# One ScalarE step of a mixture-of-experts kernel in another order: where the first part of new expert weights is split

## What is computed

```python
g = jax.lax.ragged_dot(x_sorted, we_gate, group_sizes)
u = jax.lax.ragged_dot(x_sorted, we_up, group_sizes)
o = jax.lax.ragged_dot(jax.nn.silu(g) * u, we_down, group_sizes)
w_sorted = topk_w.reshape(-1)[sort].astype(o.dtype)
y = jnp.zeros_like(x_flat).at[tok].add(o * w_sorted[:, None])
```

## Time and profile before

| | us |
|---|---|
| median of 3 runs | 3972.36 (3971.4 to 3972.74) |
| the profiled execution, as timed | 3973.47 |
| its span in the trace | 3971.7 |
| TensorE matmul busy | 3650.4 (92%) |
| VectorE busy | 2313.6 (58%) |
| ScalarE busy | 1349.9 (34%) |
| GpSimd busy | 1602.0 (40%) |

### The profile page before, as it was taken

One profiled execution on the slowest core, in us unless ns is written; L12 is line 12 of the kernel. 1 busy time (PEld: TensorE's weight loads), 2 busy tenths in 40 slices (PEclk: granted clock), 3 DMA queues, 4 the chain that ended last, 5 costly groups with the idle time before them and its releaser, 6 DMA issues.

```text
span 3971.7 us, 110141 instructions
## 1 busy us (share of the span) xinstructions
PE 3650.4 (92%) x16856; PEld 2774.8 (70%) x16857; DVE 2313.6 (58%) x5802; ACT 1349.9 (34%) x4031; POOL 1602.0 (40%) x1208
## 2 busy tenths in 40 slices
PE   6809999967999999999999999999999999999996
PEld 3404445536877777787778778787888777787785
DVE  5364555555666665656665565656555666666653
ACT  2212222213333433434333343334333343334331
POOL 1010000004555555555555455555555555455443
PEclk9959999988999999999999999999999999999998
DMA  3322323225666676667666666666666676666654
GB/s 113 106 61 86 98 97 98 96 56 122 125 154 149 153 155 122 149 127 167 141 134 127 158 137 124 138 139 152 124 127 140 122 169 153 140 133 154 137 102 74
DMA packets 216177, 502.40 MB, mean 126 GB/s; under 512 B 46587, under 2 KB 46715, under 8 KB 215360
## 3 DMA queue, kind: packets, MB, share of 16 engines
q0 software_dynamic: 129024, 320.94, 43.4%
q1 hardware_dynamic: 86592, 177.77, 13.6%
q10 hardware_dynamic: 512, 3.15, 0.3%
HBM read 1115.65 MB, written 191.41 MB: 329 GB/s over the span
## 4 chain that ended last, share of the span: by engine, by line
PE 59%; DVE 5%; issue 5%; DVEq 2%; ACT 2%; DMA 2%; ACTq 1%; POOLq 0%; POOL 0%; SPq 0%
PE e_ps_gu L1437 34%; PE e_ps_y L1456 16%; PE e_ps_x L1407 5%; DVE e_w_low L1579 3%; PE e_ps_h L1466 3%; ACT e_w_high L1516 2%; DMA out<-e_y,e_y_ids 2%; PE e_ps_find L1419 1%; DVEq L1301 1%; ACTq L1301 1%; DVE e_past L1611 1%; DVE e_y L1606 1%; DVE e_below L1622 0%; DVEq L1579 0%; ACT e_silu L1535 0%
## 5 line engine op out<-in xcount | busy, mean ns | idle before, releaser
L1381 POOL DMA_INDIRECT out<-e_y,e_y_ids x576 | 935.9, 1625 | 1326.5 <-ACT e_weight L1528 582.4
L1373 POOL DMA_INDIRECT e_x<-token_rows,e_x_ids x576 | 615.9, 1069 | 273.5 <-issue 172.7
L1437 PE MATMUL e_ps_gu<-e_w_high,e_xT_high 128*128 x2304 | 688.4, 419 | 15.1 <-issue 5.1
L1437 PE MATMUL e_ps_gu<-e_w_low,e_xT_high 128*128 x2304 | 646.6, 399 | 6.4 <-issue 4.8
L1437 PE MATMUL e_ps_gu<-e_w_high,e_xT_low 128*128 x2304 | 650.4, 401 | 0.2 <-issue 0.2
L1606 DVE TENSOR_SCALAR e_y<-e_ps_y,e_weight 128x512 f32 (+1 forms) x576 | 430.9, 748 | 243.6 <-PE e_ps_y L1456 202.9
L1587 DVE TENSOR_TENSOR e_xT_low<-e_ps_x,e_xT_high 128x512 fp32r<-128x512 f32 x576 | 397.7, 690 | 286.9 <-ACT e_xT_high L1524 173.6
L1437 PEld LDWEIGHTS e_ps_gu<-e_w_high,e_xT_low 128*128 128x128 f32 x2304 | 428.8, 189 | 128.1 <-issue 29.2
L1437 PEld LDWEIGHTS e_ps_gu<-e_w_low,e_xT_high 128*128 128x128 f32 x2304 | 428.8, 188 | 126.5 <-issue 31.1
L1535 ACT ACTIVATE e_silu<-e_ps_gu 128x256 f32<-128x256 f32 x576 | 221.2, 384 | 821.5 <-PE e_ps_gu L1437 627.0
L1437 PEld LDWEIGHTS e_ps_gu<-e_w_high,e_xT_high 128*128 128x128 f32 x2304 | 396.2, 191 | 98.1 <-issue 37.3
(11 more groups left out here) (245 smaller groups left out, 3926.0 us busy)
## 6 DMA issues: line engine op xcount, KB each, us to landing
e_w_raw<-in_L_ffn_we_gate SPq DMA_DIRECT2D x576, 512.0 KB
e_w_raw<-in_L_ffn_we_up SPq DMA_DIRECT2D x576, 512.0 KB
e_w_raw<-in_L_ffn_we_down SPq DMA_DIRECT2D x576, 512.0 KB
a_x<-in_L_attn_x SPq DMA_DIRECT2D x64, 256.0 KB, 3.4
t_x_in<-in_L_attn_x SPq DMA_DIRECT2D x64, 256.0 KB, 2.8
token_rows<-t_xn SPq DMA_DIRECT2D x64, 256.0 KB, 3.1
out<-t_y_out SPq DMA_DIRECT2D x64, 256.0 KB, 2.0
e_x<-token_rows,e_x_ids POOLq DMA_INDIRECT x576
```

Of the source, the lines that this page charges most:

```text
L1373: pool.indirect_dma_start(x[:, s % XS, :], None, k.rows, bass.IndirectOffsetOnAxis(x_ids[:, s:s + 1], 0)) \
L1381: pool.indirect_dma_start(k.out, bass.IndirectOffsetOnAxis(y_ids[:, s:s + 1], 0), y[:, s % YS, :], None, compute_op=ALU.add).then_inc(adde ...
L1437: last = nc.tensor.matmul(ps_gu[s % 2][:], x[:, s % 2, c, :], w[:, c], start=(n == 0), stop=(n == 3 * DC - 1))
```

## The change

In ScalarE's step the call of `split_high` for part 0 of tile i+2 moves from in front of part 1 and the silu to the end of the step, behind `keep_h`.

```diff
                 if exists(i + 1):
                     keep_x(i + 1, (s + 1) % SHORT, slot(1))
-                if exists(i + 2):
-                    split_high(i + 2, (s + 2) % SHORT, 0)
                 if exists(i + 1):
                     split_high(i + 1, (s + 1) % SHORT, 1)
                 activate(i, s)
                 if exists(i - 1):
                     keep_h(i - 1, (s - 1) % SHORT)
+                if exists(i + 2):
+                    split_high(i + 2, (s + 2) % SHORT, 0)
```

## The result

The changed kernel takes 4043.38 us (median of 4 runs, 4036.59 to 4046.17) against 3972.55 us for the kernel before on the same chip (4 runs, 3971.4 to 3979.07). The ratio is 1.0172, with a 95% interval of 1.0155 to 1.0190: 71 us slower. The forecast was 4061, in a range of 4015 to 4110.

What follows compares the result with a forecast made beforehand. Expert stage bound by TensorE's own work, waiting at new experts for the chain from ScalarE's `take_ids` to VectorE's low part. 3972.4 + 86 (moved copy) + 3 (skipped splits) = about 4061 us, range 4015 to 4110.

Steps and rivals of the forecast that it cites:

- The late silu cost nothing: ScalarE at new experts: silu and `keep_h` start about 1.5 us sooner in 63 steps; taken at 0 us.
- phase 0: One of four steps, 0 to 3, of the expert loop; 18 copies fall there, and the loop branches behind phase 3.
- The copy at Z + 1.2: ScalarE's part 0 copy starts at Z + 1.22, ends at Z + 3.13; by itself 0 us; possibly 0.2 earlier.
- Z: Time zero at a new expert: the start of `turn_h` (`e_ps_h`) in the step holding the copy for tile i+2.
- The sequencer stands still at the drain: ScalarE prepares what follows a `drain` only once the copy has ended, so `take_ids` starts later; forecast 4061, chance 0.80.
- the first rival: ScalarE's sequencer runs ahead during the copy, so `take_ids` starts at Z + 3.1 in every phase; 3982 us, chance 0.06.
- The preparation: ScalarE's time to ready `take_ids` behind the copy: 0.63, 1.23, 1.06 and 2.08 us by phase, plus 0.1 for the `drain`.
- L: End of VectorE's low part of the weights; forecast at Z + 7.50, 8.10, 7.93 and 9.45 in phases 0 to 3.
- What TensorE loses: At 63 new experts each delay of L counts in full before `gate_up`: 91.8 us, 86 after 6 off for overlap.
- The skipped splits: ScalarE, all 576 steps: 0.39 us each, hidden except at the loop's start, where `xT_low` loses lead; 3 us, bounds 0 to 40.
- The rival of a late loop start: Skip and `drain` cost 0.7 at the loop's start, so all 144 loops lose some 0.25 us; about 4100, chance 0.07.
- Slower, with 0.93: Chance given that the changed kernel is slower; same had 0.04 and faster 0.03.

Runs made afterwards that it cites:

- e2: Part 0's split moved to the step's end in phase 0 only, the other phases as in the kernel before; 3984.28 us, ratio 1.0022 to the kernel before.
- e7: Against the changed kernel, part 0 is split between the silu and `keep_h`; 4051.54 us, ratio 1.0195 to the kernel before.
- e5: Changed kernel, but a split really made raises the semaphore by the copy itself, with a drain only where skipped; 3969.04 us, ratio 0.9983 to the kernel before.
- e1: Part 0's split moved to the step's end in phase 3 only, the other phases as in the kernel before; 4002.18 us, ratio 1.0062 to the kernel before.
- e4: Kernel before with VectorE's `mark` moved from behind the splits to the beginning of its step; 3938.38 us, ratio 0.9907 to the kernel before.
- e9: Changed kernel with no drain behind a copy that is made and `mark` at the beginning of VectorE's step; 3935.84 us, ratio 0.9899 to the kernel before.
- e10: Kernel before with no drain behind a copy that is made and `mark` at the beginning of VectorE's step; 3928.59 us, ratio 0.9884 to the kernel before.
- e6: Kernel before, but a split really made raises the semaphore by the copy itself, with a drain only where skipped; 3964.09 us, ratio 0.9968.
- e3: Changed kernel with VectorE's `mark` moved from behind the splits to the beginning of its step; 3991.59 us, ratio 1.0039 to the kernel before.
- e8: Changed kernel with part 0 copied twice, a drain between; 4191.66 us, ratio 1.0543 to the kernel before.

## Why the prediction was right, and where it was off

*The late silu cost nothing.* Right for the change as it was made: its cure brought nothing (e2). It is not free in every order, as e7 shows: VectorE's own queue is one of two arrivals at `keep_low`, and in phase 0 it was the last one before the change.

*The copy at Z + 1.2.* It starts at Z + 0.92 (phases 1 and 3) or 1.01 (phases 0 and 2), since its branch is prepared while `keep_h` runs. I had allowed for 0.2 of that.

*The sequencer stands still at the drain.* Right, shown by e5, and the first rival with it false for this kernel.

*The preparation.* Here the sizes were off. From the copy's end to `take_ids` it is 0.90 in phases 0 to 2 (forecast 0.73, 1.33 and 1.16) and 2.17 in phase 3 (2.18). The longer idle times in the earlier trace rows were not preparation that comes again behind a drain; what they were stays open. In phase 3, from `take_ids` to L took 3.64, as in the other phases, not the 4.14 of the earlier trace rows: the 0.5 more was VectorE's own lateness behind `keep_x` (0.51 there, 0.03 now), and ScalarE's delay swallowed it. So L was forecast well in phase 0 and late by 0.64, 0.46 and 0.82 in phases 1 to 3. These three terms are the step that was mis-sized: with the L of the trace the sum is 18 x 0.43 + 17 x 0.99 + 18 x 1.28 + 10 x 1.61 = 63.7 us in place of 91.8.

*What TensorE loses.* 67.1 us are lost for 63.7 us of delay, which looks like one for one and is so in part by luck. In phases 0 and 3 it holds (7.6 for 7.7, 15.6 for 16.1), and in phase 2 1.10 are lost each for 1.28, its slack of 1.28 no shelter. In phase 1 24.0 us are lost for 16.8 of delay. About 13 of them go with the lower clock, which the rule left out, and the other 11 are fewer than the rule gives: at 14 events, where TensorE had waited 0.3 to 1.0 us for `find` before, the loss grows by about 1.05 each without the clock, and at three, where it had waited 1.8, 2.0 and 2.7 already, by nothing. So without the clock some 54 us are lost for 63.7.

*The skipped splits.* They cost nothing (0.3 us), but not for the reason given. The idle time before `take_ids` grows in every step, from 503.6 us in all to

```profile
L1544 ACT CAST e_x_ids<-e_tile_ids (+1 forms) x576 | 110.0, 192 | 861.5 <-issue 731.9
```

and inside the loop by more than the 0.39 of the forecast: in undisturbed steps from 0.40 to 1.57 us in phase 1, from 0.48 to 1.10 in phase 2 and from 0.39 to 1.43 in phase 3. That uses up most of the time that `keep_x` had waited for TensorE, before and after:

```profile
L1524 ACT CAST e_xT_high<-e_ps_x 128x512 fp32r<-128x512 f32 x576 | 336.5, 584 | 294.1 <-PE e_ps_x L1407 289.2
L1524 ACT CAST e_xT_high<-e_ps_x 128x512 fp32r<-128x512 f32 x576 | 335.8, 583 | 57.1 <-PE e_ps_x L1407 53.6
```

What shelters TensorE is the lead of `xT_low` on the next `turn_x`, still 2.5 us or more in these steps. At the loop's start the typical idle time went from 2.04 to 2.18, not by the 0.45 expected, and the lead that the forecast feared for stayed (1.79 to 1.78). The rival of a late loop start fell with it.

*Slower, with 0.93.* Right; the time came out 18 us under the forecast, nearer to it than to any rival. That it came so near owes something to two errors of opposite sign: the delays of L were put 28 us too high (91.8 for 63.7), with 6 us taken off for overlap and 3 added for the skips, and the clock's 13 us were not in the sum.

## What to carry to other kernels

When an operation is moved behind the last use of a step, look at what stands first in the next step: that is what now waits, together with the preparation that a drain exposes. With the semaphore raised by the copy itself the next instruction started 0.10 us before the end of the 1.9 us copy, and 0.35 behind it where a loop's branch came between; with a drain it was 0.90 and 2.17. And before moving anything, see what hangs on the end of the chain: here a 0.7 us instruction (`mark`) placed ahead of the long split was worth 37 us in the order before and 52 in the other.

## What the runs showed of the hardware

- At the new experts of phase 1 TensorE waited about 1.8 us for `find` (2.7 at one), and in 10 of the 17 places its granted clock was at the lower level shortly after, for about 1.3 us more of time each (3.75 against 2.43). Before the change it had waited 1.8 and 2.0 us at two of these places, with no lower clock after; in e1 both are followed by it. So a wait of this length can be followed by the lower clock and need not be. The stretches of lower clock number 1 in e4, e9 and e10, 2 before, 3 in e6, 4 in e2, e3 and e5, 7 in e1, 12 after, 18 in e7 and 48 in e8: as a rule, the longer and the more frequent the waits, the more of them. Whether the spread of the runs (10 us in the changed kernel) comes from their number isn't shown, since only one execution of each has a trace.
- ScalarE's sequencer prepares the next instructions and even the loop's branch while a 1.91 us copy runs, unless a drain follows the copy: `take_ids` starts 0.10 us before the copy's end and 0.35 behind it (e5), against 0.90 and 2.17 behind it with the drain (the changed kernel).
